# The fused attention stage of a macaron block: hi and lo values in one product, narrower score products, row sums on GpSimd, another order of work

## The reference

```python
def _L0_attn_ref(x, w_qkv, ln_w, w_proj):          # groups of 64 rows, 16 heads of 16
    qkv = jnp.einsum('bglc,cd->bgld', xg, w_qkv)
    q, k, v = jnp.split(qkv, 3, axis=-1)
    q = rmsnorm(q, ln_w); k = rmsnorm(k, ln_w)
    ...
    att = jnp.einsum('bghqd,bghkd->bghqk', q, k) * scale
    att = jnp.where(causal, att, -jnp.finfo(att.dtype).max)
    att = jax.nn.softmax(att, axis=-1)
    y = jnp.einsum('bghqk,bghkd->bghqd', att, v)
    return jnp.einsum('btc,cd->btd', y, w_proj)
...
# _L0_ffn_ref(x): a shared gated product (256 -> 2048 -> 256) plus 8 routed experts
# (256 -> 1024 -> 256), each token sent to its 2 best, at most 640 tokens an expert
x = x + 0.5 * _L0_ffn_ref(_layernorm(x), ...)
x = x + _L0_attn_ref(_layernorm(x), ...)
x = x + 0.5 * _L0_ffn_ref(_layernorm(x), ...)
```

## Time and profile before

| what | value |
|---|---|
| time, median of 3 runs | 2207.35 us (2206.16 to 2208.19) |
| time of the profiled execution | 2215.33 us |
| its span in the trace | 2213.3 us |
| mean granted TensorE clock | 0.995 |
| PE busy | 2169.2 us (98%) |
| PEld busy | 2005.1 us (91%) |
| DVE busy | 1366.4 us (62%) |
| ACT busy | 1037.1 us (47%) |
| POOL busy | 437.3 us (20%) |

### The profile page before, as it was taken

The page is one execution under the profiler, slowest core; times in us unless marked ns, Lnnn a source line. Parts: engine busy times, 40 slices in busy tenths (PEclk is TensorE's granted clock), DMA queues, the critical chain, the costliest instruction groups (busy, mean ns, idle before and its releaser), DMA issues.

```text
span 2213.3 us, 38807 instructions
## 1 busy us (share of the span) xinstructions
PE 2169.2 (98%) x14464; PEld 2005.1 (91%) x14464; DVE 1366.4 (62%) x3182; ACT 1037.1 (47%) x2004; POOL 437.3 (20%) x424
## 2 busy tenths in 40 slices
PE   7999999999999999999999999999999999999999
PEld 6888889999998899999998898888899999988887
DVE  6666546666665676777778786666466666533333
ACT  3233335555553666666666663333355555432222
POOL 2323211122112221122222232332112121200000
PEclk9999999999999999999999999999999999999999
DMA  9231224554445000000101101312244444441010
GB/s 271 94 106 56 72 60 128 133 149 100 101 105 153 20 3 18 20 20 1 34 1 49 44 11 56 118 64 72 61 101 105 109 101 101 106 133 58 29 58 20
DMA packets 194490, 168.42 MB, mean 76 GB/s; under 512 B 16905, under 2 KB 175037, under 8 KB 194304
## 3 DMA queue, kind: packets, MB, share of 16 engines
q1 hardware_dynamic: 176640, 144.57, 21.9%
q0 software_dynamic: 17664, 21.38, 5.6%
HBM read 104.32 MB, written 68.07 MB: 78 GB/s over the span
## 4 chain that ended last, share of the span: by engine, by line
PE 88%; DVE 7%; issue 2%; ACT 1%; DMA 1%; another core or an unknown queue 1%; SPq 0%; POOL 0%; DVEq 0%; ACTq 0%; POOLq 0%
PE gate_up_p L327 29%; PE quad L327 26%; PE out_p L365 20%; PE misc L365 4%; PE misc L495 3%; PE quad L512 3%; DVE h_s L967 1%; PE misc L391 1%; PE misc L383 1%; PE misc L402 1%; PE misc L400 0%; DVE y_s L1093 0%; DVE hl L971 0%; DMA stage<-in_L_ffn_rd 0%
## 5 line engine op out<-in xcount | busy, mean ns | idle before, releaser
L327 PE MATMUL gate_up_p<-zh,w 128*128 128x512 f32 (+2 forms) x2368 | 707.6, 362 | 2.4 <-DVE zl L839 2.3
L646 ACT CAST hh<-h_s 128x512 fp32r<-128x512 f32 (+2 forms) x512 | 277.4, 542 | 655.1 <-DVE h_s L967 621.3
L365 PE MATMUL out_p<-w,hh 128*128 128x256 f32 x2816 | 563.8, 282 | 6.0 <-DVE hl L971 5.3
L327 PE MATMUL quad<-zh,w 128*128 128x512 f32 (+2 forms) x1728 | 484.2, 348 | 0.0
L327 PEld LDWEIGHTS gate_up_p<-zh,w 128*128 128x128 f32 x2368 | 431.2, 189 | 54.5 <-DVE zl L839 2.8
L365 PEld LDWEIGHTS out_p<-w,hh 128*128 128x128 f32 x2816 | 458.6, 189 | 19.3 <-DVE hl L971 9.0
L327 PE MATMUL gate_up_p<-zl,w 128*128 128x512 f32 (+2 forms) x1184 | 423.7, 358 | 0.0
L365 PE MATMUL out_p<-w,hl 128*128 128x256 f32 x1408 | 394.1, 280 | 0.0
L327 PEld LDWEIGHTS quad<-zh,w 128*128 128x128 f32 x1728 | 309.9, 189 | 27.2
L971 DVE TENSOR_TENSOR hl<-h_s,hh 128x512 fp32r<-128x512 f32 (+2 forms) x432 | 247.8, 574 | 137.7 <-ACT hh L646 117.7
L967 DVE TENSOR_TENSOR h_s<-gate_up_p,sg_s 128x512 f32<-128x512 f32 (+2 forms) x296 | 178.2, 602 | 232.7 <-PE gate_up_p L327 218.3
(11 more groups left out here) (168 smaller groups left out, 2868.3 us busy)
## 6 DMA issues: line engine op xcount, KB each, us to landing
stage<-in_L_ffn_rg SPq DMA_DIRECT2D x128, 128.0 KB
stage<-in_L_ffn_ru SPq DMA_DIRECT2D x128, 128.0 KB
stage<-in_L_ffn_rd SPq DMA_DIRECT2D x128, 128.0 KB
slots_d<-empty SPq DMA_DIRECT2D x16, 662.5 KB, 7.8
zh_d<-zh SPq DMA_DIRECT2D x16, 512.0 KB
zl_d<-zl SPq DMA_DIRECT2D x16, 512.0 KB
y_d<-x SPq DMA_DIRECT2D x16, 512.0 KB
zh<-zh_d SPq DMA_DIRECT2D x16, 512.0 KB, 4.3
```

The lines of the kernel that those rows point to most:

```text
L327: last = pe.matmul(dst, a, b, start=(k == 0), stop=(k == 3 * n - 1))
L365: last = pe.matmul(out[:, j // 2, o:o + C], a[:, par, cols], w[:, hi, :], start=(c == 0 and i == 0 and j % 2 == 0), stop=(c == NCH - 1 and ...
L646: nc.scalar.copy(hh[:, n % 2, 0:ncol], h_s[:, n % 2, 0:ncol]).then_inc(sm["hh_done"], 1)
```

## The change

Within the fused stage:

- `values`: high and low values lie side by side in one tile `vv`; the high probabilities multiply both at once (128 columns), the low ones only the high values (64 columns): 16 matmuls in place of 24. The columns of ones are gone.
- The softmax sums come from GpSimd instead: `row_sums_half` (three additions of 128x256) and `row_sums` (four small ones), into `den_a`. The two column blocks of a product are added by VectorE with two `tensor_reduce`; a reciprocal of 128x16 and one multiplication follow.
- `scores`: of each pair of matmuls the second loads 66 instead of 128 columns of weights; `qcat` and `kcat` are transposed with 112 instead of 128 columns.
- TensorE's order in a step: transposes of the normed tile before those of the output (with a new wait, `a_ysum`); the down product of the chunk before moves ahead of the `p_s` transposes, `up(n)` behind them; `up(n+1)` ahead of `prep`.
- ScalarE: `h_high(n)` ahead of `twin`.
- VectorE: in steps with c > 0, `stats` and `normal` move to the start of the step; with c = 0 both stand between `add_shared` and `masked`. `extras(s-1, 1)` moves ahead; `outputs` and `extras(s, 0)` move ahead of `fused_low(n+1)`. `masked` also waits for `a_half`.
- GpSimd: the pieces' low parts of steps 29 to 32 (128x768 each, two a step) come from VectorE; `root` moves to the start of the step when c > 0; the low parts of q and k move behind the subtraction of the maximum.

Outside it: in the last expert block SP issues `load_z(f, "s1", 0)` behind the second of four `load_piece` instead of ahead of the first. `itok` shares memory with the start-up weights, and three memsets are added in step 3.

```diff
+            def pair_transposes(src, rows, done):
...
-                    last = pe.transpose(misc[:, j // 4, (j % 4) * P:(j % 4 + 1) * P],
-                                        src[:, 2 * j:2 * j + 2, :].rearrange("p h d -> p (h d)"), ident[:, :])
+                    last = pe.transpose(misc[0:rows, j // 4, (j % 4) * P:(j % 4 + 1) * P],
+                                        src[:, 2 * j:2 * j + 2, :].rearrange("p h d -> p (h d)")[:, 0:rows], ident[:, :])
...
-                    for g in range(2):
+                    for g, rows in ((1, P), (0, GROUP + 2)):
...
-                        last = pe.matmul(quad[:, j // 4, o:o + P].rearrange("p (r c) -> p r c", r=2), q_t[:, j, g, :],
-                                         k_t[:, j, :, own], start=(g == 0), stop=(g == 1))
+                        last = pe.matmul(quad[0:rows, j // 4, o:o + P].rearrange("p (r c) -> p r c", r=2), q_t[:, j, g, 0:rows],
+                                         k_t[:, j, :, own], start=(g == 1), stop=True, skip_group_check=(g == 0))
...
-                    o = (j % 4) * 66
-                    last = split_product(quad[:, j // 4, o:o + 66], [(ph[:, j, :], pl[:, j, :], vh[:, q, j, :], vl[:, q, j, :])], 1)
+                    o = (j % 4) * P
+                    pe.matmul(quad[:, j // 4, o:o + P], ph[:, j, :], vv[:, q, j, :, :].rearrange("p a c -> p (a c)"), start=True, stop=False)
+                    last = pe.matmul(quad[:, j // 4, o:o + 64], pl[:, j, :], vv[:, q, j, 0, :], start=False, stop=True)
...
-                    pair_transposes(qcat, "a_qt")
+                    pair_transposes(qcat, QKROWS, "a_qt")
+                if z is not None:
+                    if out is not None:
+                        pe.wait_ge(sm["a_ysum"], out + 1)
+                    z_transpose(z)
...
-                if z is not None:
-                    z_transpose(z)
...
-                    pair_transposes(kcat, "a_kt")
+                    pair_transposes(kcat, QKROWS, "a_kt")
...
-                up(n, b % 2, c, buf, SB)
+                down_of(*chunk_before(f, phase, b, c))
...
-                    pair_transposes(p_s, "a_pt")
-                down_of(*chunk_before(f, phase, b, c))
+                    pair_transposes(p_s, P, "a_pt")
+                up(n, b % 2, c, buf, SB)
...
+                up(n + 1, b % 2, c + 1, buf, SB)
...
-                up(n + 1, b % 2, c + 1, buf, SB)
...
             def outputs(t):
...
-                yp = quad[:, :, 0:4 * 66].rearrange("p b (j c) -> p b j c", c=66)
-                rd4 = rden[:, :].rearrange("p (b j r) -> p b j r", b=2, r=2)
-                for b in range(2):
-                    last = v.reciprocal(rd4[:, b, :, :], yp[:, b, :, 64:66])
-                last.then_inc(sm["a_rden"], 1)
-                dve.wait_ge(sm["a_rden"], t + 1)
+                yp = quad[:, :, :].rearrange("p b (j a c) -> p (b j) c a", a=2, c=64)
+                dve.wait_ge(sm["a_den"], t + 1)
+                v.reciprocal(rden[:, :], den_a[:, :]).then_inc(sm["a_rden"], 1)
...
-                    for b in range(2):
-                        src = yp[rows, b, :, 32 * g:32 * g + 32].rearrange("p j (r d) -> p j r d", d=HD)
-                        dst = y_s[rows, :].rearrange("p (b j r d) -> p b j r d", b=2, r=2, d=HD)[:, b]
-                        last = v.tensor_tensor(dst, src, rd4[rows, b].unsqueeze(3).broadcast_to([64, 4, 2, HD]), ALU.mult)
-                last.then_inc(sm["a_yn"], 1)
+                    last = v.tensor_reduce(y_s[rows, :].rearrange("p (j c) -> p j c", c=2 * HD), yp[rows, :, 32 * g:32 * g + 32, :], AX, ALU.add)
+                last.then_inc(sm["a_ysum"], 1)
+                dve.wait_ge(sm["a_rden"], t + 1)
+                dve.wait_ge(sm["a_ysum"], t + 1)
+                y_heads = y_s[:, :].rearrange("p (h d) -> p h d", d=HD)
+                v.tensor_tensor(y_heads, y_heads, rden[:, :].unsqueeze(2).broadcast_to([P, NH, HD]), ALU.mult).then_inc(sm["a_yn"], 1)
...
             def extras(s, second):
...
-                c += second
-                prep(*prep_block(f, phase, b), c)
-                refill = c - 2 if phase == "s1" and b == NB - 1 else c + NCH - 2 if phase == "s0" and b == 0 else -1
-                if 0 <= refill < NCH:
-                    piece_low(1, 0, refill)
+                prep(*prep_block(f, phase, b), c + second)
...
             def fused_step(s):
...
+                if ahead is not None and c:
+                    stats(ahead)
...
+                if s == 0:
+                    half_low(0, NEB - 1, NCH - 1)
+                else:
+                    extras(s - 1, 1)
+                if ahead is not None and c:
+                    normal(ahead)
...
-                if s == 0:
-                    half_low(0, NEB - 1, NCH - 1)
-                else:
-                    extras(s - 1, 1)
...
-                if ahead is not None:
+                if ahead is not None and c == 0:
...
+                    normal(ahead)
...
-                if ahead is not None:
-                    normal(ahead)
-                fused_low(n + 1)
...
+                fused_low(n + 1)
...
+
+            def row_sums_half(t):
+                pool.wait_ge(sm["a_exp"], t + 1)
+                g.tensor_tensor(psums[:, :, :], p_s[:, :, 0:HD], p_s[:, :, HD:2 * HD], ALU.add).then_inc(sm["a_tree"], 1)
+                pool.wait_ge(sm["a_tree"], 5 * t + 1)
+                g.tensor_tensor(psums[:, :, :], psums[:, :, :], p_s[:, :, 2 * HD:3 * HD], ALU.add).then_inc(sm["a_tree"], 1)
+                pool.wait_ge(sm["a_tree"], 5 * t + 2)
+                g.tensor_tensor(psums[:, :, :], psums[:, :, :], p_s[:, :, 3 * HD:GROUP], ALU.add).then_inc(sm["a_half"], 1)
+
+            def row_sums(t):
+                pool.wait_ge(sm["a_half"], t + 1)
+                for level, wide in ((3, HD // 2), (4, HD // 4), (5, HD // 8)):
+                    g.tensor_tensor(psums[:, :, 0:wide], psums[:, :, 0:wide], psums[:, :, wide:2 * wide],
+                                    ALU.add).then_inc(sm["a_tree"], 1)
+                    pool.wait_ge(sm["a_tree"], 5 * t + level)
+                wait(pool, sm["a_rden"], t)
+                g.tensor_tensor(den_a[:, :], psums[:, :, 0], psums[:, :, 1], ALU.add).then_inc(sm["a_den"], 1)
+
+            def root(t):
+                m = t % 2
+                pool.wait_ge(sm["av"], 3 * t + 3)
+                g.tensor_tensor(ard[:, m:m + 1], ave[:, m:m + 1], mhalf[:, 0:1], ALU.pow).then_inc(sm["a_rs"], 1)
+
+            def piece_low(j):
+                pool.wait_ge(sm["wh_done"], piece_of(1, 0, j) + 1)
+                w = W[buf_of(1, 0)]
+                g.tensor_tensor(w[:, 1, j, :], stage[:, j % 2, :], w[:, 0, j, :], ALU.subtract).then_inc(sm["wl_done"], 1)
...
             def fused_step(s):
...
-                z, keys, ahead = (tile_at(s, stage) for stage in ("z", "keys", "stats"))
+                z, keys, ahead, probs = (tile_at(s, stage) for stage in ("z", "keys", "stats", "probs"))
...
+                if ahead is not None and c:
+                    root(ahead)
+                if probs is not None:
+                    row_sums_half(probs)
...
-                if ahead is not None:
-                    m = ahead % 2
-                    pool.wait_ge(sm["av"], 3 * ahead + 3)
-                    g.tensor_tensor(ard[:, m:m + 1], ave[:, m:m + 1], mhalf[:, 0:1], ALU.pow).then_inc(sm["a_rs"], 1)
+                if probs is not None:
+                    row_sums(probs)
+                if ahead is not None and c == 0:
+                    root(ahead)
+                if keys is not None:
+                    pool.wait_ge(sm["a_max"], keys + 1)
+                    g.tensor_tensor(p_s[:, 0:HALF, :], p_s[:, 0:HALF, :],
+                                    smax[:, 0:HALF].unsqueeze(2).broadcast_to([P, HALF, GROUP]), ALU.subtract).then_inc(sm["a_sub0"], 1)
...
-                if keys is not None:
-                    pool.wait_ge(sm["a_max"], keys + 1)
-                    g.tensor_tensor(p_s[:, 0:HALF, :], p_s[:, 0:HALF, :],
-                                    smax[:, 0:HALF].unsqueeze(2).broadcast_to([P, HALF, GROUP]), ALU.subtract).then_inc(sm["a_sub0"], 1)
+                refill = c - 2 if phase == "s1" and b == NB - 1 else c + NCH - 2 if phase == "s0" and b == 0 else -1
+                if 0 <= refill < NCH:
+                    piece_low(refill)
+                    piece_low(refill + 1)
...
             def ln(f, k):
...
-                    if b == NEB - 1:
-                        load_z(f, "s1", 0)
...
+                        if b == NEB - 1 and jj == 1:
+                            load_z(f, "s1", 0)
...
```

39 lines of the change are left out of this document (21 added, 18 removed).

## The result

The changed kernel takes 2214.85 us (median of 7, 2213.63 to 2222.01), the kernel before 2207.66 on the same chip (7, 2206.16 to 2211.27). The ratio is 1.0034 [1.0024, 1.0044]: 7 us slower, where 34 us faster was forecast. The forecast had the wrong sign, and the time lies outside its range.

A forecast was written before the change was run, and what follows sets the result against it. TensorE, busy 98% of the span, was taken as the bound. Gains of 22.4, 0.6, 12.4 and 6.0 us less 7.2 made 34 us, so 2173 us from a median of 2207.35; range 2150 to 2199.

The forecast's parts named there:

- load_z: Last expert block: issuing it behind two pieces removes waits and a clock fall, 6 us saved, bounds 0 and 6.3.
- c > 0 steps, 7 to 27: Fused-stage steps with c > 0: 16 of them gain 1.4 us each, 22.4 us in all.
- c = 0 steps, 8 to 28: Fused-stage steps with c = 0: six of them lose 1.2 us each, 7.2 us in all.
- late part, from 29: Steps 29 to 38: 12.4 us gained, including half of TensorE's 10.5 us of waits.
- steps 2 to 4: Early fused steps: no gain or loss in the sum; the added memsets were counted at nothing.
- Row sums and reductions: GpSimd's 128x256 additions, 0.75 us each, counted at nothing; VectorE's reductions some 0.65 us, giving VectorE 0.5 to 0.6 us more work.
- rival B: `outputs` on VectorE becomes the bound: strided reductions take 1.22 us, costing 20 us, total 2193 us; chance 0.12.
- The transposes: TensorE: 16 transposes with loads of 112 instead of 128 columns save 0.22 us a step.
- The chain through GpSimd: From `up(n)` through two low parts of 0.75 us: 7.5 us against TensorE's 7.38, so about 0.1 us of waiting.
- My section on the port: GpSimd and VectorE both on SBUF: VectorE's subtraction loses some 0.25 us; at most 8 us over 32 steps.
- rival C: Every step TensorE stops 0.7 us before the `qcat` transposes and the clock falls, 1.34 us: 2238 us, slower; chance 0.09.
- The memsets: Added memsets on VectorE: cost nothing, since VectorE has idle time there.

The follow-up runs named there:

- e4: The kernel before with one edit: `load_z` of the first s1 block issued behind the second `load_piece` of the last expert block; 2200.16 us, ratio 0.9969 to the kernel before.
- e3: The changed kernel with GpSimd's low parts of q and k ahead of the subtraction of the maximum again; 2208.55 us, ratio 1.0004 to the kernel before.
- e1: The changed kernel with VectorE's normalization behind the subtraction again in c = 0 steps; 2200.74 us, ratio 0.9971 to the kernel before.
- e10: e9 with the second pieces behind the `k_t` copy (e6) and the three memsets at the start of step 4 (e12); 2178.07 us, ratio 0.9883 to the kernel before.
- e6: The changed kernel with the second pieces, `extras(s-1, 1)`, back behind the `k_t` copies in VectorE's order; 2207.5 us, ratio 1.001 to the kernel before.
- e9: The changed kernel with the orders of both e1 and e3; 2190.23 us, ratio 0.9934 to the kernel before.
- e12: The changed kernel with the three added memsets at the start of step 4 instead of step 3; 2208.75 us, ratio 1.0015 to the kernel before.
- e7: The changed kernel without GpSimd's softmax row sums, two tiny additions in their place, so denominators are left out; 2205.23 us, ratio 1.0001 to the kernel before.

## Why the prediction was wrong

| term | forecast | measured against e4 |
|---|---|---|
| `load_z` | -6.0 | -6.8 (e4) |
| c > 0 steps, 7 to 27 | -22.4 | -13.0 |
| step 6 | -0.6 | +0.2 |
| c = 0 steps, 8 to 28 | +7.2 | +12.1 |
| late part, from 29 | -12.4 | +8.0 |
| steps 2 to 4 | 0 | +7.2 |

**Right.** `load_z`, its place and its size. The 16 `values` matmuls take 1.70 us (959.63 to 961.33 below), 0.106 each, against 2.59 for 24: the wider product costs nothing. The score products take 1.41 us (1.37 forecast). Row sums and reductions have the durations taken (0.75 and 0.66 us each), and no c > 0 step from 9 to 25 waits for `y_s`, so rival B was wrong. The extra time of c = 0 steps was sized well too (below). TensorE after, `values` and the wait behind the down matmuls:

```profile
959.63 0.22 PE L528 MATMUL quad<-vv,ph 128*128 128x128 f32 x1
...
961.33 0.36 PE L367 MATMUL out_p<-w,hh 128*128 128x256 f32 x1
...
963.13 1.08 PE L497 MATMUL misc<-ident,qcat 128*112 128x128 f32 x8 [0.18 <-POOL kcat L1297]
```

**The c > 0 step, off by 0.45 us.** Two terms of the sum were mis-sized. (a) The transposes, 0.22 us: loads of 112 columns brought nothing, 8 for `kcat` take 0.79 us after, from 966.59 to the next instruction at 967.38, and 0.79 us before (912.75 to 913.54). The stream without waits is the 17.63 us of e3, not 17.36: 18.87 - 0.89 - 0.40 = 17.58. (b) The chain through GpSimd: I took both low parts at 0.75 us, from rows where they ran beside VectorE's mask. Now the first runs beside VectorE's subtraction. That is slow in all 32 steps, and the low part takes 1174 ns in the mean (before: 679 ns at best, and 747 ns):

```profile
L1296 POOL TENSOR_TENSOR qcat<-qk,qcat 128x256 fp32r<-128x256 f32 x32 | 37.6, 1174 | 4.5 <-ACT kcat L708 4.5
...
L1248 POOL TENSOR_TENSOR psums<-p_s 128x256 f32<-128x256 f32 x32 | 23.9, 745 | 12.9 <-ACT p_s L757 12.9
```

```profile
L1087 DVE TENSOR_TENSOR p_s<-p_s,smax x32: 929/932/936, 733.9 to 1347.6; 128x512 f32<-128x512 f32 x32
```

My section on the port priced VectorE's side of this (0.25 us) and forgot GpSimd's (0.43 us), which was in the chain. e3, which takes the low parts out of this chain, shows the price of their place: 0.3 us a step; how much of it is the slower instruction was not run apart. This is near rival C's mechanism, with under half of the 0.7 us it took for the stop and without its fall of the clock. C had the sign right, but its stop in every step was small; the stops of 2 us came in every fourth. The Trainium skill, "GPSIMD Engine Reference" (section 1), says that GpSimd shares its SBUF interfaces with VectorE and that VectorE instructions with two SBUF inputs contend for them. The rows agree, for both sides.

**The c = 0 step.** Its chain was seen and sized: from `h_s` to the mask 4.83 us were measured (4.72 forecast), and with the clock up the `qcat` transposes start 3.10 us later in the step than with c > 0 (14.24 us in step 28, 11.14 in step 18), where the forecast had 3.0. To charge this delay once, at the end of the chain, was right: the stop for the mask comes first, but it and the fall behind it only take the place of a wait for `kcat`. The fall costs 0.37 us; 0.5 us had been put down. So 17.95 + 3.10 + 0.37 = 21.4 us, against 20.5 + 0.5 = 21.0. The six steps together are 5.2 us above the forecast: 2.6 us from the same 0.45 us as with c > 0, 1.6 from the second fall in step 8, and 1.0 from step 28, which waits 1.14 us for x. The order ahead of the mask was forecast as a loss of 7.2 us; e1 takes 1.1 us of that delay out of each step.

**The late part.** This is the term that failed by most and that turned the sign. The two sums of the table are 42 us apart, and 20.4 us of that lie here, 9.4 in the c > 0 steps, 7.2 in steps 2 to 4, 4.9 in the c = 0 steps. With -12.4 for the late part the changed kernel would have been 13 us faster than the kernel before; with any one of the other terms as forecast it would lie between 2 us faster and 3 us slower.

I expected half of the 10.5 us of waits to go because VectorE gave work away. From step 29 on TensorE's waits grew instead, from 9.4 us in e4 to 17.5, and VectorE's busy time by 15.4 us (the two windows above). The low parts of the pieces are gone (7.6 us), but `outputs` takes 2.1 us a tile, not 1.25, so 0.8 us more where the forecast had 0.5 to 0.6. And the short routing instructions (111 in this stretch, 4 to 64 elements a row) take 33.8 us together against 20.0, where they stand beside GpSimd's work, as in step 32 above; in e10 they take 24.0. Step 32, which the forecast put at nothing, is 28.20 us long and was 23.36 in e4; TensorE stops in it for the mask (1.90 us) and for `y_s` (2.06 us). The order of VectorE's queue has its share: the second `prep` work ahead of the normalization (e6: 4.2 us of steps 29 to 35), and the low parts of q and k last on GpSimd (e9 reads 5.5 us less than e1 there, from its fast execution). In e10, with the same instructions, VectorE's busy time is 173.4 us and the late part 2.4 us shorter than e4's. So even in the better order the term is -2.4, not -12.4.

**Priced at nothing.** The memsets: "VectorE has idle time there" was read from the share of idle time, not from the instruction behind them; they cost 3.7 us (e12). In step 4, also c = 0, the statistics ahead of `hl` cost another 2.7 us (e1), where the forecast did not look, since only the first tile's statistics stand there. The row sums cost 7 us in the changed order and nearly nothing in e10's.

**What stays open.** The waits for x are 4.5 of e7's 7 us; the rest was not traced. It was not tried whether another order gets at the 11.4 us that e10 still waits for `y_s`. What makes the clock fall behind some stops and not behind others is not shown: of two stops of 2.06 us, in steps 24 and 28 of one trace, only the first was followed by a fall.

## What to carry to other kernels

When a chain is put on an engine's queue, list every semaphore of it that TensorE waits for. A stop at an early one is not added to the wait at the last, and neither is all of a fall of the clock between them: here a fall cost 0.4 us where a later wait would have come anyway, and 1.5 us where none did. Before work is moved between two engines, sum the busy time of both in the stretch with the durations that they have beside each other: here VectorE gave away 7.6 us and was busy 15.4 us longer. Changes of the arithmetic and of the order should be timed apart: here the same arithmetic (with `load_z` moved) was worth 26 us in one order, and four places of the order written with it cost 33. "The engine is idle there" counts only when the instruction queued behind is shown to have the time.
